# Second attention layer of a two-layer cross-attention kernel: two heads at a time in the two row halves of the array, and masks shared among four engines

## What is computed

```python
q = hidden_state @ Wq + bq                      # (4, 512, 512)
k = encoder_hidden_state @ Wk + bk              # (4, 1601, 128)
v = encoder_hidden_state @ Wv + bv
scores = jnp.einsum('bkgld,bksd->bkgls', q, k) * scale
scores = scores + encoder_attention_mask[:, :, None, :, :]   # (4, 1, 512, 1601)
attn = jax.nn.softmax(scores, axis=-1)
out = jnp.einsum('bkgls,bksd->bkgld', attn, v)
out = out.transpose(0, 3, 1, 2, 4).reshape(b, l, H)
out = out @ Wo + bo
x = out + hidden_state                          # then a layer norm with gamma, beta
```

## Time and profile before

| what | value |
|---|---|
| median of three runs | 4313.34 us (4313.16 to 4319.02) |
| profiled execution | 4312.53 us, span 4310.7 us |
| mean granted TensorE clock | 0.959 |
| busy share of the span | TensorE 91%, VectorE 65%, ScalarE 55%, GpSimd 50% |
| first batch, layer 0 and `middle` | 0 to 606 us |
| first batch, layer 1 | 606.6 us (first matmul) to 1072 us (last output issued) |

### The profile page before, as it was taken

The page is one execution under the profiler, slowest core; times in us unless marked ns, Lnnn a source line. Parts: engine busy times, 40 slices in busy tenths (PEclk is TensorE's granted clock), DMA queues, the critical chain, the costliest instruction groups (busy, mean ns, idle before and its releaser), DMA issues. The chain is left out here.

```text
span 4310.7 us, 55881 instructions
## 1 busy us (share of the span) xinstructions
PE 3924.4 (91%) x17920; PEld 2002.0 (46%) x17920; DVE 2803.3 (65%) x7505; ACT 2355.7 (55%) x2828; POOL 2159.6 (50%) x1020
## 2 busy tenths in 40 slices
PE   8999899997899989999789998999978999899997
PEld 4444664443444466444334446644434444664442
DVE  3555459995355545999535554599963555459995
ACT  0546238885054623888505452388860546238885
POOL 0657127774065712777505561177750657127774
PEclk9999989998899998999889999899999999989999
DMA  4112321110411232111041123211104112421110
GB/s 116 41 41 46 139 75 29 30 28 15 115 41 41 46 137 77 29 30 28 15 115 41 41 45 137 77 28 30 29 15 115 41 41 46 139 75 29 30 28 15
DMA packets 115783, 240.67 MB, mean 56 GB/s; under 512 B 26245, under 2 KB 47493, under 8 KB 106761
## 3 DMA queue, kind: packets, MB, share of 16 engines
q1 hardware_dynamic: 111048, 231.54, 21.5%
q10 hardware_dynamic: 4416, 5.30, 0.5%
HBM read 117.17 MB, written 4.19 MB: 28 GB/s over the span
## 5 line engine op out<-in xcount | busy, mean ns | idle before, releaser
L947 POOL TENSOR_TENSOR l_pt<-l_pt,l_maskT 128x1024 f32<-128x1024 f32 x512 | 1220.4, 2395 | 486.3 <-ACT l_pt L965 486.3
L1001 DVE CUSTOM_DVE_ANT_0 tile_b<-l_psR,hT 128x400 f32<-128x400 f32 (+1 forms) x2048 | 1076.3, 569 | 108.5 <-PE l_psR L1083 107.9
L398 DVE TENSOR_REDUCE l_acc<-l_psR 128x1 f32<-128x424 f32 (+1 forms) x1280 | 706.0, 591 | 468.1 <-PE l_psR L478 460.1
L975 ACT ACTIVATE l_pt<-l_pt 128x1024 f32<-128x1024 f32 (+1 forms) x896 | 877.3, 993 | 25.4 <-POOL l_pt L947 5.3
L1083 PE MATMUL l_psR<-split_w,qst 128*128 128x400 f32 (+1 forms) x2048 | 760.6, 412 | 64.2 <-PEq L1186 23.2
L370 ACT ACTIVATE l_pt<-l_psB 128x1024 f32<-128x1024 f32 (+1 forms) x576 | 549.6, 977 | 290.8 <-PE l_psB L500 238.2
L1083 PEld LDWEIGHTS l_psR<-split_w,qst 128*128 128x128 f32 x2048 | 381.3, 195 | 681.6 <-DVE l_acc L1001 584.4
L965 ACT ACTIVATE l_pt<-l_psB 128x1024 f32<-128x1024 f32 x512 | 523.2, 1022 | 108.4 <-PE l_psB L1105 105.3
L1105 PE MATMUL l_psB<-qst,split_w 128*128 128x512 f32 (+1 forms) x1664 | 556.2, 410 | 9.6 <-ACT l_pt L965 5.7
L1116 PE MATMUL l_psO<-l_pt,V 128*32 128x512 f32 (+1 forms) x3328 | 543.9, 607 | 18.0 <-ACT l_osb L987 10.1
L478 PE MATMUL l_psR<-l_kst,l_qst 128*128 128x424 f32 (+1 forms) x1280 | 478.6, 420 | 66.1 <-issue 46.6
(11 more groups left out here) (139 smaller groups left out, 4275.8 us busy)
## 6 DMA issues: line engine op xcount, KB each, us to landing
l_kst<-l_khl SPq DMA_DIRECT2D x192, 264.1 KB, 3.8
mid_w<-in_w SPq DMA_DIRECT2D x128, 256.0 KB, 3.5
qst<-q SPq DMA_DIRECT2D x512, 32.0 KB, 2.0
qst<-qlast SPq DMA_DIRECT2D x128, 128.0 KB, 2.3
hT<-in_maskN SPq DMA_DIRECT2D x16, 800.5 KB, 11.1
split_w<-k SPq DMA_DIRECT2D x128, 100.1 KB, 3.6
l_qst<-l_qhl SPq DMA_DIRECT2D x192, 64.0 KB, 2.0
l_maskT<-in_maskT SPq DMA_DIRECT2D x48, 256.0 KB
```

What stands on the lines that cost most here:

```text
L398: dve.tensor_reduce(acc[:, h % 2, qt, c:c + 1], psR[:, ring[item] % NR, 0:w], AX.X, ALU.max).then_inc(s_red, 1)
L947: pool.tensor_tensor(tile, tile, maskT[:, kt:kt + 2, :].rearrange("p a n -> p (a n)"), ALU.add)\
L975: act.activation(pt[0:r, n % NPT1, 0:w], pt[0:r, n % NPT1, 0:w], ACT.Exp).then_inc(s_exp, 1)
L1001: dve.tensor_tensor_reduce(junk[:, n % 2, 0:hi - lo], psR[:, ring[item] % NR, 0:hi - lo], maskN[:, qt, lo:hi], 1.0, -3e38, ALU.add, ALU.ma ...
```

## The change

Layer 1 works on pairs of heads, 16 pairs. The two heads of a pair have a stack of 64 rows each: head 2p in partitions 0 to 63, head 2p+1 in 64 to 127. A stack has three products of 16 rows and the maximum's two rows at 32 and 33 (or 96 and 97). Two matmuls, one on each half of the rows, take the place of two matmuls over 128 rows; A writes two banks, B the two halves of one step, which is now one key tile for both heads, 13 steps a pair. W handles two key tiles of two heads in its four column groups.

Masks: of the 13 key tiles five are masked by TensorE ("p": identity times the mask, split in high and low parts, for both heads, 4 matmuls more a step; ScalarE then takes the exponential from PSUM), seven by ScalarE's copy and GpSimd ("a"), the last by VectorE ("d"). The masks for TensorE are bounded and split at the layer's start by GpSimd and ScalarE, and lie in two new float32r buffers. E, Y and X handle four pairs where they had eight heads; O is four items. VectorE's steps get names of their own (T for the maximum, N for all four small reductions, Z for the last product).

The order of the list comes from a list scheduler (`plan_layer1`) that keeps a clock in its own units for each engine and picks, by rank, the first item that is ready. The key stack takes 6 copies, the pair of queries 8. Maxima may run two pairs ahead of the scores (`AHEAD`). The main parts of the diff, with headings in place of line numbers:

```diff
-NPT0, NPT1 = 4, 6
+NPT0, NPT1 = 4, 7
-POOL_PAIRS = (0, 1, 3, 5)
+PAIRS_OF_HEADS = H1 // 2
+MASKED_BY, LAST_BY, LAST_PAIRS = "paapapapapaad", "paapapapapaad", 1
+PE_KT = [kt for kt in range(T1) if MASKED_BY[kt] == "p"]
+LOWEST = -3e38
+RANK = {"PE": "MYXaBWAO", "DVE": "NZDTR", "ACT": "JESCP", "POOL": "G"}
+LENGTH = {"A": 20, "T": 50, "M": 40, "B": 27, "mask": 94, "W": 102, "D": 114, "C": 94, "P": 94, "J": 103, "E": 52, "G": 234, "N": 55, "Y": 52, "S": 55, "R": 86, "X": 52, "Z": 60, "O": 260}
+LATER = {"PE": 23, "DVE": 15, "ACT": 16, "POOL": 11}
+AHEAD, FEW = 2, 3
...
 def plan_layer1():
...
+    def slot(x):
+
+        i = index[x] - NPT1
+        return i < 0 or done("W", score[i][0], score[i][1] // 2 * 2)
+
+    def ready(k, x):
+        if k in took and not bank():
+            return False
+        if k == "A":
+            return (x[0] < 2 or done("N", x[0] - 2)) and x[0] <= (todo["B"] or [(pairs,)])[0][0] + AHEAD
...
+        if k == "B":
+            return done("J", x[0]) and (index[x] < 2 or done(*left(score[index[x] - 2])))
...
+        if k == "O":
+            return not todo["B"] and done("Z", pairs // 4 - 2) and all(done(*left(x)) for x in score[-4:])
...
+    while any(todo.values()):
...
+            for engine, rank in RANK.items():
+                if free[engine] > now:
+                    continue
+                waiting = sum(1 for x in ring[-NR:] if not done(*x))
+                for k in rank:
+                    if k == "a":
+                        k = "A" if waiting < FEW else ""
+                    options = todo.get(k, [])[:12 if k == "P" else 1]
+                    x = next((x for x in options if ready(k, x)), None)
...
+                    length = LENGTH[k] + (LENGTH["mask"] if k == "B" and mode[x] == "p" else 0)
+                    if k == "A" and x[3] and partner == ("A", *x[:3], 0):
+                        length = 2
...
+                    free[engine] = now + length
+                    ends[(k, *x)] = now + length + LATER[engine]
+                    plan.append((k, *x))
...
@@ middle, SyncE @@
-        sp.wait_ge(s_h, NF)
-        for kv in range(2):
-            copy_keys(sp, kst, k1, kv, s_k1)
-        sp.wait_ge(s_last, 7)
+        sp.wait_ge(s_last, 6)
+        copy_keys(sp, kst, k1, 0, s_k1)
+        sp.wait_ge(s_last, 8)
         sp.wait_ge(s_split, kq[("Q", 0)])
-        for h in range(SLOTS):
-            copy_queries(sp, qst, q1, qlast, h, s_stack)
+        for p in range(2):
+            copy_queries(sp, qst, q1, kst, p, s_stack)
+        copy_keys(sp, kst, k1, 1, s_k1)
+        for p in range(2, SLOTS):
+            copy_queries(sp, qst, q1, kst, p, s_stack)
@@ middle, VectorE, after the x1 additions @@
-        dve.memset(qlast[64:128, :].bitcast(F32), 0.0).then_inc(s_last, 1)
-        for i in range(2):
-            dve.memset(kst[64:128, i, :].bitcast(F32), 0.0).then_inc(s_last, 1)
-            dve.memset(kst[0:64, i, N1:N1 + 1].bitcast(F32), 0.0).then_inc(s_last, 1)
-        dve.wait_ge(s_last, 5)
-        for i in range(2):
-            dve.memset(kst[96:98, i, :].bitcast(F32), 1.0).then_inc(s_last, 1)
+        for lo in (32, 96):
+            dve.memset(kst[lo:lo + 32, :, :].bitcast(F32), 0.0).then_inc(s_last, 1)
+            dve.memset(kst[lo - 32:lo, :, N1:N1 + 1].bitcast(F32), 0.0).then_inc(s_last, 1)
+        dve.wait_ge(s_last, 4)
+        for lo in (32, 96):
+            dve.memset(kst[lo:lo + 2, :, :].bitcast(F32), 1.0).then_inc(s_last, 1)
+        for lo in (32, 96):
+            dve.memset(qst[lo:lo + 32, :, :].bitcast(F32), 0.0).then_inc(s_last, 1)
@@ copies @@
+    for half in (0, 64):
+        for row, part in ((0, 0), (16, 1), (48, 0)):
+            sp.dma_start(kst[half + row:half + row + 16, kv % 2, 0:N1].bitcast(F32),
+                         k1[16 * kv:16 * kv + 16, part, :].bitcast(F32)).then_inc(s_k[kv % 2], 16)
...
+    for e in range(2):
+        h = 2 * p + e
+        for row, part in ((0, 0), (16, 0), (48, 1)):
+            sp.dma_start(qst[64 * e + row:64 * e + row + 16, s, :].bitcast(F32),
+                         q1[16 * (h % 8):16 * (h % 8) + 16, h // 8, part, :].bitcast(F32)).then_inc(s_stack[s], 16)
+        sp.dma_start(qst[64 * e + 32:64 * e + 34, s, :].bitcast(F32),
+                     kst[34:36, 0, 0:L].bitcast(F32)).then_inc(s_stack[s], 16)
@@ layer 1, SyncE @@
+        for p in range(PAIRS_OF_HEADS - 2):
+            sp.wait_ge(s_b, bb[("B", p, T1 - 1)])
+            if p % 2 and (p + 3) // 2 < KV1:
+                copy_keys(sp, kst, k1, (p + 3) // 2, s_k)
+            if p + SLOTS < PAIRS_OF_HEADS:
+                copy_queries(sp, qst, q1, kst, p + SLOTS, s_stack)
@@ layer 1, GpSimd @@
+        for i, t in enumerate(PE_KT):
+            r = rows(t, N1)
+            pool.wait_ge(s_mt[t], 16)
+            pool.tensor_scalar(raw[i][0:r, :], raw[i][0:r, :], LOWEST, None, ALU.max).then_inc(s_low, 1)
+        for i, t in enumerate(PE_KT):
+            r = rows(t, N1)
+            pool.wait_ge(s_mhi, i + 1)
+            pool.tensor_tensor(maskP[0:r, 1, i, :], raw[i][0:r, :], maskP[0:r, 0, i, :].bitcast(F32), ALU.subtract)\
+                .then_inc(s_mlo, 1)
...
+                pool.tensor_tensor(probabilities(n, r), probabilities(n, r), mask_of(t, r), ALU.add).then_inc(s_padd, 1)
@@ layer 1, ScalarE @@
+                for lo in (32, 96):
+                    act.activation(qst[lo:lo + 2, p % SLOTS, :], bank(at)[lo:lo + 2, :], ACT.Copy).then_inc(s_rows, 1)
...
+                act.activation(probabilities(n, r), scores(n, r), ACT.Copy).then_inc(s_copy, 1)
...
+                if at in by_pe:
+                    act.wait_ge(s_b, n)
+                    if n > NPT1:
+                        act.wait_ge(s_pv, n - NPT1)
+                    act.activation(probabilities(n, r), scores(n, r), ACT.Exp).then_inc(s_exp, 1)
@@ layer 1, VectorE @@
+                dve.tensor_tensor(probabilities(n, r), scores(n, r), mask_of(item[2], r), ALU.add).then_inc(s_add, 1)
@@ layer 1, TensorE @@
+                pe.matmul(bank(item)[:, 0:CH1[c + 1] - CH1[c]], qst[half, s, qt * P:(qt + 1) * P],
+                          kst[half, kv % 2, CH1[c]:CH1[c + 1]], start=True, stop=True).then_inc(s_a, 1)
...
+                for e in range(2):
+                    half = slice(64 * e, 64 * e + 64)
+                    mm = pe.matmul(psB[0:r, 2 * (n % 2) + e, :], kst[half, kv % 2, t * P:t * P + r], qst[half, s, :],
+                                   start=True, stop=item not in by_pe, skip_group_check=True)
+                for part in range(2 * (item in by_pe)):
+                    for e in range(2):
+                        mm = pe.matmul(psB[0:r, 2 * (n % 2) + e, :], ident[0:r, 0:r], maskP[0:r, part, PE_KT.index(t), :],
+                                       start=False, stop=part == 1, skip_group_check=True)
...
+                    for e in range(2):
+                        q = 2 * (x % 2) + e
+                        mm = pe.matmul(psO[32 * q:32 * q + 32, :], V1[0:r, x, kv, :], pt[0:r, n % NPT1, 512 * e:512 * e + 512],
+                                       start=(x < 2), stop=(x >= T1 - 2), skip_group_check=True)
...
+                for j in range(4):
+                    mm = pe.matmul(bank(item)[32 * j:32 * j + 32, :], sel[:, 1 + (k == "Y"), :], osb[j],
+                                   start=True, stop=True, skip_group_check=True)
```

More of the change, by code:

```diff
@@ L1119, in _ @@
[L1119 to L1128 removed]
+                _, p, t = item
+                kv, burst = p // 2, range(t, min(t + 2, T1))
```

366 lines of the change are left out of this document (201 added, 165 removed).

## The result

Eight runs of the changed kernel gave a median of **4296.6 us** (4288.3 to 4299.0), eight of the kernel before 4313.1 (4306.3 to 4319.0): ratio 0.9963, 95% interval 0.9952 to 0.9973. That is 16.6 us less where the prediction had 118 less. All readings are again of the first batch.

What follows compares the result with a forecast made beforehand. VectorE was taken as the bound before, TensorE and ScalarE as joint bounds after. Terms of -52.8, +20.4, +1.5, +1.5, -8 and +8 gave -29.4 us per batch, four times -118: 4312.5 - 118 = 4195 us, range 4080 to 4330.

Steps and rivals of the forecast that it cites:

- steady stage: Layer 1 from first ScalarE copy to last exponential: 22.3 us per two heads instead of 25.6, -52.8 us per batch.
- border: Ahead of layer 1: longer clears and 44 copy issues instead of 28 delay the barrier, +20.4 us per batch.
- fill: Start of layer 1: a second copy of the maximum's rows and the first tile's masks, +1.5 us per batch.
- tail: End of layer 1: output projection in four pieces behind W and a shorter Y, -8 us per batch.
- semaphores: Between batches: clearing 15 new semaphores, +1.5 us per batch.
- stops for keys: Layer 1: TensorE's queue waits at an even pair's A for late key copies, two stops of 4 us, +8 per batch.
- TensorE's sum: Layer 1: TensorE's work per two heads after the change, added from pitches to 21.5 us.
- price of a change of tiling: TensorE in layer 1: 0.27 - 0.18 = 0.09 us for each of 26 changes per two heads.
- fill of 0.96: Layer 1's steady running: assumed busy share of TensorE, turning 21.5 us into a period of 22.3 us.
- reading of the bound: Steady running before the change: VectorE, busy 92.6%, is the bound; TensorE's 341.0 us don't count as such a number.
- VectorE's lead: Layer 1: maxima's lead over scores grows by 3 us a pair, reaching two pairs at about pair 8.
- Rival (b): Border and stops eat the gain: period 23.5 from in-order stalls, three full stops +13, 4304 us; chance 0.10.

Runs made afterwards that it cites:

- e1: Changed kernel with TensorE's masks added in 64-row halves, high part twice, low part left out; 4207.3 us, ratio 0.975.
- e5: Changed kernel with one overwritten four-column full-array matmul before the scores of each tile that ScalarE and GpSimd mask; 4427.9 us.
- e6: Changed kernel with both heads' A and B matmuls reading rows 0 to 63, the odd heads' scores left out; 4706.5 us.
- e10: e7 with e9's tiles, high and low mask parts, three of four mask tiles in halves, six probability buffers instead of seven; 4280.7 us, ratio 0.992.
- e12: e10 with the scheduler holding an even pair's maxima until five scores of the pair two before are out; 4216.4 us, ratio 0.977.
- e2: Changed kernel with the copies of keys 1 and of the queries of pairs 2 and 3 issued behind the barrier; 4242.5 us, ratio 0.983.
- e7: e2 with GpSimd clearing one of the two row groups while VectorE clears the other; 4215.6 us, ratio 0.978.
- e4: Changed kernel with the masks of two tiles moved from TensorE to VectorE, order worked out anew; 4438.3 us, ratio 1.029.
- e9: e1 with four tiles masked by TensorE instead of five, and eight by ScalarE and GpSimd instead of seven; 4221.8 us.
- e15: e12 with seven probability buffers and two instead of three mask tiles in row halves, nothing left out; 4158.7 us, ratio 0.965.
- e13: e12 with seven probability buffers, all four mask tiles in halves, low mask part left out; 4128.6 us, ratio 0.957.
- e14: e13 with six probability buffers instead of seven; 4214.1 us, ratio 0.977.

## Why the prediction was wrong

Faster was right and the value lay in the range, but the gain was a seventh of the forecast. Per batch, from the first batch of the profiled executions:

| term | predicted | measured | from |
|---|---|---|---|
| steady stage | -52.8 | -26.9 | 409.6 to 382.7 |
| border | +20.4 | +23.8 | start of the x1 additions to first matmul, 23.9 to 47.7 |
| fill | +1.5 | +4.6 | first matmul to first ScalarE operation, 19.2 to 23.8 |
| tail | -8 | -7.7 | last exponential to last scaling, 33.6 to 26.0 |
| semaphores | +1.5 | +1.2 | last output issued to next batch, 12.1 to 13.4 |
| stops for keys | +8 | 0 | no such wait in the trace |
| the rest | 0 | -1.2 | layer 0 and `middle` |
| sum | -29.4 | -6.2 | 1084.4 to 1078.2 |

Over all four batches the span fell by 18.2, 4.6 a batch. Border, fill and stage are within 1.5 us of the table in every batch; the tail gained less in the third and fourth, where the kernel before took 30.6 us from the last exponential to the last scaling and not 33.6.

**The step that failed is TensorE's sum, 21.5 us, and in it above all the price of a change of tiling, "0.27 - 0.18 = 0.09".** The runs put it at 0.13 to 0.16 us on the period and 0.2 in single starts. That difference of two starts holds only what the next group pays at the switch. It leaves out that the group's second weight load comes late. With the terms as they measured: 16 A pairs x 0.18 + 13 B pairs x 0.23 + 20 mask matmuls x 0.235 + W 6.4 + M, Y and X 0.7 = 17.7, and 24 changes x 0.2 = 4.8, together 22.5; over a fill of 0.96, 23.4. That is the period of a plain pair. The pairs were cheaper than taken (0.18 for 0.22, 0.23 for 0.25), and the prediction's 1.00 for a W burst, from the start of the W to the start of the A behind it, held a change that its sum counted again; so errors of opposite sign stood in the sum. e1 and e5 show the changes on the path in both directions; e6 shows the overlap of the halves.

That the new sum meets 23.4 is partly luck. The 0.96 was never measured by itself, and 0.2 is a little high in the mean, since a change into W costs 0.11. And one term stands in neither sum: the list doesn't keep the two heads together. In 74 of its 256 places the first matmul of an A pair is followed by another item and not by its partner. In three plain periods of the trace (670.67 to 740.85 us) 11.0 pairs of A and 6.3 pairs of B a period start together, 6.3 times an A starts beside a B, and 11.0 matmuls stand alone: 34.7 places for the 29 of the sum. At 0.18 and 0.23 us a place that is an estimated 1.2 us a pair. How much of the miss is each term's is open; e1 and e5 measure the changes alone.

Against the forecast's 22.3 stands the mean, 23.9: the three pairs with Y and X take 2.0 us more, and each pair behind them 0.6. The prediction had no wait for them. Yet some 9 of the 26.9 us that the stage gained came from there, since the kernel before lost 5.7 us at each. Besides, 21.5 / 0.96 is 22.4; "rounded down" to 22.3 it gave the forecast 1.6 us a batch.

The Trainium skill (TensorEngine Tiling (Array Packing), Key Properties) says that a change of the tiling mode drains the engine. The prediction wrote that 0.09 us agrees; the rule gives no price, and the runs put it at 0.13 to 0.2. A rule without a price had been weighed as if one row settled it.

**The reading of the bound failed with it.** The prediction set TensorE's 341 of 350 us aside and took VectorE alone as the bound. Added up from single starts in the same way, the kernel before comes to 20.3 us without changes and 20.3 + 16.3 x 0.2 = 23.6 us with them, for two heads: level with VectorE's 23.7. This is argued from the terms and no run of the kernel before was made for it. A change that takes work from VectorE and gives TensorE eight more changes and 20 mask matmuls could then only win by the overlap. The 128.8 us that weight loads waited for VectorE didn't speak against that: the changed kernel, held by TensorE, still shows 83.6.

**The stops for keys** failed on another step. The prediction let VectorE's lead grow while the kernel runs; but the order is fixed in the list before it runs. There nine B steps stand between the score whose end starts the key copies and the first A that needs them, for every even pair from 4 to 14, and the lead stays about one pair. This could be read off the list. The mechanism itself is right: in e10's list there are 8, 5, 5, 2, 2 and 2 such steps, and its trace has 12.0 us in three waits in the stretch looked at; e12 keeps at least five, and one wait of 0.8 us is left.

**The border** was right in kind and in its parts (keys ready at 598, the last issue forecast at 626, found at 628). Measured from the x1 additions, which stood 1.2 us earlier, it came out 3.4 us longer: the four clears of 3204 columns came 3.45 apart where 3.1 was taken (1.4 in all), and the 38 issues behind the queries' clears took 25.6 us, 0.67 each for 0.63 (1.7). e2 and e7 show that nothing covered it: with most of it removed 81 us come back.

**The fill** came out 3.1 longer than forecast. M stands 18.4 us behind the first matmul, where it stood 16.4 behind it before, and the first four mask matmuls take 2.07 us at the lower clock (granted 0.50), where 0.92 was taken. ScalarE's table load (1.28 us) isn't the cause: it is over at 651.0, and ScalarE then waits 1.92 us for these masks. **The tail** came as said: one piece of O stands between the last W, and the last W starts at 1038.35, 2.8 us after the last exponential, where it had been 11.5.

Rival (b), 4304, came nearest in time, and its period of 23.5 nearly met the measured 23.9; but it reached it by in-order stalls, and it counted 13 us of stops for keys of which none came. Its nearness is in good part luck.

## What to carry to other kernels

Count the changes of tiling in TensorE's queue and price each from the start of the group before it to the second start behind it; here some 0.13 to 0.2 us. 24 of them took 3 to 4.8 us of a pair, about the 4.0 that the overlap of the row halves is worth by e6. Put work of one tiling together, or bring the odd operation into the tiling around it, as the masks in halves do. Where the order comes from a scheduler, read its own period, and the distance from each copy to its first reader, off the list before a run: e4's loss and the long pairs of e9 and e12 to e15 stood there. And where a step needs more issues before a barrier, look first at what can be issued behind it: the issues that only the third pair needed had cost 54 us.

## What the hardware showed that was not expected

- Row halves overlap: the second of a pair starts 0.003 us after the first, and a pair that stands together costs what one matmul costs (0.18 us to the next pair of A, 0.23 of B). The Trainium skill (TensorE: Matmul & The Clock Gate, Part 3, The mechanism) puts such starts 4 ns apart; the trace agrees. The same section's rule that a weight load overlaps a running matmul only when the row group differs is not what these traces show in running on one tiling: full-array mask matmuls of one row group keep 0.235 us from start to start with a load each. (In the text above the rule the section also lets a load for the background weight buffer go ahead, which fits.) Only just behind a change does the second start come late, at 0.333.
- Busy shares of 81% for VectorE and ScalarE and 92% for TensorE went together with a mean period of 26.15 us in e4, where the kernel before needed 25.3 for two heads.
- One buffer of probabilities of seven was worth 85 us (e13 against e14), with an order worked out for each number; GpSimd's additions lie between ScalarE's copy and its exponential.
- Where the work of TensorE stopped for some microseconds, the next group ran at the lower of its two clocks: W 1.93 us in e10 behind a stop of 3.11 us, 1.06 otherwise.

Open: what part of e4's loss the clock had; what each term of TensorE's sum had of the miss; whether the list with its A pairs kept together would gain the estimated 1.2 us a pair; whether the low part of the mask in halves for all four tiles with seven buffers would reach e13's time, which was not tried for lack of room.
